# Local attention layers of a three-stage kernel: score products over a stacked high and low part of q, laid out by DMA, and the value matmuls of a tile in one run

## The reference

```python
h = shift_token(x)                       # second half of the features from the token before
q, k, v = jnp.split(h @ wqkv, 3, axis=-1)            # 8 heads of 64
q, k = l2norm(q) * qs, l2norm(k) * ksc
q, k = rotary_xpos(q, k)
# windows of 128 tokens: a query sees the keys of its own window and of the one before
sim = jnp.einsum('bhwid,bhwjd->bhwij', bq * 8, look_around(bk))
attn = softmax(where(mask, -max, sim))
x = x + (attn @ look_around(bv)) @ wo
```

## Time and profile before

| | |
|---|---|
| time, 3 runs | 6484.46, 6486.76, 6487.22 us, median 6486.76 |
| the profiled execution: its own time, its span | 6483.36 us, 6481.6 us |
| mean granted TensorE clock over the span | 0.981 |
| first stage | 0 to 3577 us |
| local attention of layer 0 and 1 | 3577 to 4595, 5039 to 6043 us |
| feed-forward of layer 0 and 1 | 4595 to 5039, 6043 to 6481 us |
| TensorE, VectorE, ScalarE, GpSimd busy over the span | 95%, 79%, 59%, 26% |

### The profile page before, as it was taken

The page is one execution under the profiler, slowest core; times in us unless marked ns, Lnnn a source line. Parts: engine busy times, 40 slices in busy tenths (PEclk is TensorE's granted clock), DMA queues, the critical chain, the costliest instruction groups (busy, mean ns, idle before and its releaser), DMA issues. The chain is left out here.

```text
span 6481.6 us, 108848 instructions
## 1 busy us (share of the span) xinstructions
PE 6166.7 (95%) x41920; PEld 3444.3 (53%) x42112; DVE 5091.6 (79%) x10817; ACT 3803.7 (59%) x6226; POOL 1699.0 (26%) x1259
## 2 busy tenths in 40 slices
PE   6999999999999999999999799999899899999899
PEld 2333333333333333333233688888788688888788
DVE  5877888877888878888886788888666788888666
ACT  1666665666656666656666566666333566666332
POOL 3011000001000100000000577777100577777111
PEclk7999999999999999999999899999999899999999
DMA  2001101111001110010000100000100100000111
GB/s 84 21 29 34 33 16 40 31 29 36 21 30 31 34 32 26 21 37 21 16 16 19 39 15 13 15 14 10 28 11 4 34 15 14 13 15 9 54 50 43
DMA packets 161677, 170.60 MB, mean 26 GB/s; under 512 B 26844, under 2 KB 146436, under 8 KB 161156
## 3 DMA queue, kind: packets, MB, share of 16 engines
q1 hardware_dynamic: 161156, 163.62, 8.9%
HBM read 104.04 MB, written 41.94 MB: 23 GB/s over the span
## 5 line engine op out<-in xcount | busy, mean ns | idle before, releaser
L533 ACT ACTIVATE a_pr<-a_w 128x1024 f32<-128x1024 f32 x2048 | 2078.4, 1024 | 1145.4 <-PE a_w L421 825.8
L637 DVE TENSOR_REDUCE a_mx<-a_b 128x1 f32<-128x512 f32 x2688 | 1740.2, 685 | 326.5 <-PE a_b L405 307.4
L405 PE MATMUL a_b<-a_kp,a_qp 96*128 96x512 bf16 x4096 | 1445.2, 387 | 111.7 <-DVE a_mx L637 48.6
L421 PE MATMUL a_w<-a_qp,a_kp 99*128 99x512 bf16 x4096 | 1225.3, 380 | 33.7 <-ACT a_pr L533 33.6
L635 DVE CUSTOM_DVE_ANT_0 a_junk<-a_b,a_gw 128x512 bf16<-128x512 f32 x1408 | 965.7, 686 | 246.6 <-PE a_b L405 206.9
L452 PE MATMUL a_po<-a_pr,a_v 128*17 128x512 f32 x8192 | 1067.8, 594 | 0.5 <-ACT a_pr L533 0.5
L405 PEld LDWEIGHTS a_b<-a_kp,a_qp 96*128 96x128 bf16 x4096 | 335.3, 97 | 1255.5 <-issue 701.1
L1378 POOL TENSOR_TENSOR l_p<-l_p,l_rc 128x512 f32<-128x512 f32 (+1 forms) x512 | 632.5, 1254 | 450.8 <-DVE l_rc L1291 450.8
L1185 ACT ACTIVATE l_p<-l_S,l_nm 128x256 f32<-128x256 f32 (+1 forms) x1024 | 467.8, 466 | 457.8 <-DVE l_nm L1283 457.6
L421 PEld LDWEIGHTS a_w<-a_qp,a_kp 99*128 99x128 bf16 x4096 | 388.3, 98 | 521.3 <-ACT a_pr L533 110.8
L1034 PE MATMUL l_G<-l_wqkv,l_hT 128*128 128x512 f32 x2304 | 606.9, 408 | 22.0 <-DVE l_wqkv L1323 9.5
(11 more groups left out here) (163 smaller groups left out, 8222.0 us busy)
## 6 DMA issues: line engine op xcount, KB each, us to landing
a_qp<-q_parts SPq DMA_DIRECT2D x384, 64.0 KB, 2.3
a_kp<-k_parts SPq DMA_DIRECT2D x384, 64.0 KB, 2.2
a_xc<-in_x SPq DMA_DIRECT2D x32, 512.0 KB
l_tab<-in_rotary SPq DMA_DIRECT2D x128, 128.0 KB, 2.1
q_parts<-a_stage SPq DMA_DIRECT2D x32, 384.0 KB, 2.5
k_parts<-a_stage SPq DMA_DIRECT2D x32, 384.0 KB, 2.6
x<-a_xc SPq DMA_DIRECT2D x16, 512.0 KB, 2.9
f_xo<-x SPq DMA_DIRECT2D x16, 512.0 KB
```

Source lines behind the costliest of these rows:

```text
L405: eng.matmul(bk, qp[s][0:96, qb * 128:qb * 128 + 128], kp[s][0:96, c * 512:c * 512 + 512], start=True, stop=True).then_inc(full, 1)
L421: m = eng.matmul(wide[u][:, c * 512:c * 512 + 512], kp[s][0:99, kb * 128:kb * 128 + 128], qp[s][0:99, u * 1024 + c * 512:u * 1024 + c * 51 ...
L533: eng.activation(pr[(2 * n + u) % NP][:, :], wide[u][:, :], ACT.Exp, scale=0.25).then_inc(s_exp[u], 1)
L637: t = eng.tensor_reduce(mx[g % 2][:, qb, c:c + 1], banks[i], X, ALU.max)
```

## The change

Scores: q is laid out anew for each head, its 64 high rows over its 64 low rows (`qs`). The keys are laid out as `kh`, the high part twice, once beside each half of q, and `kl`, the low part beside the high half of q with zeros below it. One matmul with `kh` then gives (high + low) by high, and one with `kl` high by low. Each covers one head and both windows of keys, so a pair of heads takes four matmuls of 256 columns where it took six. Keys of three tiles lie in three slots; where the slots of the two windows come in turned order, `place` says so and a second, turned mask is used.

ScalarE and VectorE now write all of q and k in one instruction each to plain buffers `qT` and `kT` (one of each, not two or three), and SyncE copies them from there to the stacked buffers: `stack(t, 0)` issues 4 DMAs and `stack(t, 1)` issues 6, each of 64 partitions by 4 x 128 numbers (128 KB). `sim` waits for the 4 of q and the 6 of k. `hT` and `oT` are one buffer instead of two.

Values: the four `pv` of a tile now follow `out` at the end of TensorE's step. Output: `out` makes high by high and high by low with 4 matmuls of 512 columns and low by high with 4 of 256 (before 12 of 256), and VectorE adds the two halves to `xs` in two instructions.

```diff
+    qT, kT = [sb(f"qT{k}", [128, 4, 128], F32R) for k in range(2)], [sb(f"kT{k}", [128, 4, 128], F32R) for k in range(2)]
+    qs = [sb(f"qs{i}", [128, 4, 2, 128], F32R) for i in range(2)]
+    kh, kl = (sb(n, [128, 4, 2, 3, 128], F32R) for n in ("kh", "kl"))
...
-            pe.wait_ge(s_ql, t + 1)
-            pe.wait_ge(s_kl, t + 1)
-            for k in ([0, 1] if w else [1]):
-                for x, y in PASSES:
-                    m = eng.matmul(z[:, :, k, :], qT[t % 2][x][:, pair * 128:pair * 128 + 128], kT[(t - 1 + k) % 3][y][:, pair, :, :],
+            pe.wait_ge(s_qs[t % 2], 64 * (t // 2 + 1))
+            pe.wait_ge(s_ks[t % 3], 96 * (t // 3 + 1))
+            slots = [t % 3] if not w else [0, 2] if t % 3 == 0 else [t % 3 - 1, t % 3]
+            step = slots[-1] - slots[0] or 1
+            for x in (kh, kl):
+                for h in range(2):
+                    m = eng.matmul(z[:, h, 0:2, :] if w else z[:, h, 1, :], qs[t % 2][:, pair, h, :],
+                                   x[:, pair, h, slots[0]:slots[-1] + 1:step, :] if w else x[:, pair, h, slots[0], :],
                                    start=False, stop=True, skip_group_check=True)
...
-            for x, z in PASSES:
-                for c in range(4):
-                    m = eng.matmul(G[1][:, 0:D], oT[t % 2][x][:, c * 128:c * 128 + 128], wo[z][:, c, :], start=i == 0, stop=i == 11)
-                    i += 1
+            for c in range(4):
+                eng.matmul(G[1][:, :], oT[0][:, c * 128:c * 128 + 128], wo[:, c, :, :].rearrange("p z n -> p (z n)"),
+                           start=c == 0, stop=True, skip_group_check=True)
+            for c in range(4):
+                m = eng.matmul(G[1][:, 0:D], oT[1][:, c * 128:c * 128 + 128], wo[:, c, 0, :], start=False, stop=True, skip_group_check=True)
...
             on(p_T, n - 3, 1)
-            on(pv, n - 3, 0)
             on(qk_T, n - 1, 1)
             on(p_T, n - 3, 2)
             on(p_T, n - 3, 3)
-            on(pv, n - 3, 1)
             on(sim, n - 2, 3)
             on(x_T, n + 1)
-            on(pv, n - 3, 2)
             on(out, n - 4)
-            on(pv, n - 3, 3)
+            for pair in range(4):
+                on(pv, n - 3, pair)
...
-            eng.tensor_tensor(xs[:, t, :], G[1][:, 0:D], xs[:, t, :], ALU.add).then_inc(s_res, 1)
+            eng.tensor_tensor(xs[:, t, :], G[1][:, 0:D], xs[:, t, :], ALU.add).then_inc(s_half, 1)
+            dve.wait_ge(s_half, t + 1)
+            eng.tensor_tensor(xs[:, t, :], G[1][:, D:2 * D], xs[:, t, :], ALU.add).then_inc(s_res, 1)
...
-        for x in [x for both in kT for x in both]:
-            m = eng.tensor_scalar(x[:, :, :, :].rearrange("p a h n -> p (a h) n"), ident[:, :].unsqueeze(1).to_broadcast([128, 8, 128]), 0.0, None, ALU.mult)
+        for o in range(4):
+            m = eng.tensor_scalar(kl[64:128, o, :, :, :].rearrange("p h s n -> p (h s) n"),
+                                  ident[64:128, :].unsqueeze(1).to_broadcast([64, 6, 128]), 0.0, None, ALU.mult)
...
+        def stack(t, n):
+
+            sp.wait_ge(s_kl if n else s_ql, t + 1)
+            if t > 1:
+                sp.wait_ge(s_sim, 4 * (t - 2) + 4)
+            for h in range(2):
+                rows = slice(64 * h, 64 * h + 64)
+                if n:
+                    s = t % 3
+                    for r in range(2):
+                        eng.dma_start(kh[64 * r:64 * r + 64, :, h, s, :].bitcast(F32), kT[0][rows, :, :].bitcast(F32)).then_inc(s_ks[s], 16)
+                    eng.dma_start(kl[0:64, :, h, s, :].bitcast(F32), kT[1][rows, :, :].bitcast(F32)).then_inc(s_ks[s], 16)
+                else:
+                    for r in range(2):
+                        eng.dma_start(qs[t % 2][64 * r:64 * r + 64, :, h, :].bitcast(F32), qT[r][rows, :, :].bitcast(F32)).then_inc(s_qs[t % 2], 16)
...
+            if n:
+                stack(n - 1, 0)
+                stack(n - 1, 1)
             if n + 2 < NT:
                 load_table(n + 2)
```

More of the change, by code:

```diff
@@ L959, in local_layer @@
     wq = [sb(f"wqkv{i}", [128, 2, 3 * HL * DL], F32R) for i in range(2)]
-    wo = [sb(f"wo{i}", [128, 4, D], F32R) for i in range(2)]
+    wo = sb("wo", [128, 4, 2, D], F32R)
     tab = [sb(f"tab{i}", [128, 2, 2, DL]) for i in range(3)]
@@ L963, in local_layer @@
     ident, identb = sb("ident", [128, 128]), sb("identb", [128, 128], BF16)
-    mask = sb("mask", [128, 512], BF16)
+    mask = [sb(f"mask{i}", [128, 2, 2, 128], BF16) for i in range(2)]
     nh = sb("nh", [128, 16])
     sh = [sb(f"sh{i}", [128, 4, 128]) for i in range(2)]
-    hT = [[sb(f"hT{i}{k}", [128, 256], F32R) for k in range(2)] for i in range(2)]
+    hT = [sb(f"hT{k}", [128, 256], F32R) for k in range(2)]
     qk = sb("qk", [128, 2, HL, DL])
@@ L978, in local_layer @@
     pT = [sb(f"pT{i}", [128, 2, 2, 128]) for i in range(4)]
-    oT = [[sb(f"oT{i}{k}", [128, 512], F32R) for k in range(2)] for i in range(2)]
+    oT = [sb(f"oT{k}", [128, 512], F32R) for k in range(2)]
     G = [ph.ps(f"G{i}", [128, 512]) for i in range(2)]
@@ L986, in local_layer @@
     mask32, wraw = sq[:, 0, :, :].rearrange("p h d -> p (h d)"), t1[1][:, :, :, :].rearrange("p a h d -> p (a h d)")
-    wo_flat = [x[:, :, :].rearrange("p a n -> p (a n)") for x in wo]
+    wraw_c = wraw.rearrange("p (c n) -> p c n", n=D)
     s_ident, s_cq, s_cw = ph.sem("ident"), ph.sems("cq", 2), ph.sem("cw")
@@ L999, in local_layer, with place @@
     n_zero = sum(1 for g in range(NT // 4) if 4 * g % W == 0)
+    def place(t, k):
+        return 1 - k if t % W and t % 3 == 0 else k
     def pos(pairs, t, pair):
@@ L1033, in qkv @@
                 for c in range(2):
-                    m = eng.matmul(G[n % 2][:, :], hT[t % 2][x][:, c * 128:c * 128 + 128], wq[z][:, c, n * 512:n * 512 + 512], start=i == 0, stop=i == 5)
+                    m = eng.matmul(G[n % 2][:, :], hT[x][:, c * 128:c * 128 + 128], wq[z][:, c, n * 512:n * 512 + 512], start=i == 0, stop=i == 5)
                     i += 1
@@ L1162, in qk_hi @@
             act.wait_ge(s_qkT, 2 * t + n + 1)
[L1163 to L1173, removed]
+            d, full = (kT, s_kh) if n else (qT, s_qh)
+            if t:
+                if n:
+                    act.wait_ge(s_ks[(t - 1) % 3], 96 * ((t - 1) // 3 + 1))
+                else:
+                    act.wait_ge(s_qs[(t - 1) % 2], 64 * ((t - 1) // 2 + 1))
+            eng.activation(d[0][:, :, :].rearrange("p a n -> p (a n)"), T[:, :], ACT.Copy).then_inc(full, 1)
         def sim(t, pair):
@@ L1329, in vector @@
                 dve.wait_ge(s_cw, 48)
-                eng.tensor_copy(mask[:, :], mask32).then_inc(s_mask, 1)
+                for i in range(2):
+                    for k in range(2):
+                        m = eng.tensor_copy(mask[i][:, :, k, :], mask32.rearrange("p (h k n) -> p h k n", h=2, k=2)[:, :, k ^ i, :])
+                m.then_inc(s_mask, 1)
                 dve.wait_ge(s_woh, 1)
-                eng.tensor_tensor(wo_flat[1], wraw, wo_flat[0].bitcast(F32), ALU.subtract).then_inc(s_wol, 1)
+                eng.tensor_tensor(wo[:, :, 1, :], wraw_c, wo[:, :, 0, :].bitcast(F32), ALU.subtract).then_inc(s_wol, 1)
             on(sim, n - 2, 1)
@@ L1419, in sync @@
         load_wqkv(2)
-        for n in range(NT):
+        for n in range(NT + 1):
             g = (n + 4) // 4
```

50 lines of the change are left out of this document (25 added, 25 removed).

## The result

| | before | after |
|---|---|---|
| median of 4 runs each, us | 6485.61 (6481.80 to 6487.22) | 7171.77 (7168.29 to 7175.56) |
| span of the profiled execution, us | 6481.6 | 7173.8 |
| mean granted clock of TensorE | 0.981 | 0.932 |

The ratio is 1.1059, 95% interval 1.1045 to 1.1073: 10.6% slower, 686 us. The forecast was 6872 us, the range ended at 7080. The sign and the mechanism came as predicted, the size did not: 386 us were forecast, and the measured time lies above the range.

What follows compares the result with a forecast made beforehand. TensorE's stream was taken to set the 15.15 us step, then the chain through k's copies: 12.43 + 4.7 = 17.1 us. 126 x (1.95 + 1.05 for the clock) plus 7 adds 385 us: 6872 us, range 6650 to 7080.

Steps and rivals of the forecast that it cites:

- TensorE's own work falls by 0.94 us a step: Score matmuls per tile go from 24 to 16 at 0.117 us each; TensorE's work falls from 15.15 to 14.21 us.
- `out` gives nothing: Output product on TensorE: the new matmuls take 1.40 us, as the 12 before did, so no gain.
- The chain takes over: From k's landing through `qkv`, ScalarE's copy and VectorE's list to the end of k's low part: 12.43 us.
- T: The moment when a tile's k has landed and its first score products start on TensorE; a turn was forecast at 17.1 us.
- The landing, 4.7 us: SyncE's six DMAs behind the low part of k: 5 x 0.50 + 2.1 + 0.1 us, bounds 3.9 and 6.7.
- the 3.8 us: Cross-check of the landing by the skill's formula: the six copies taken as one transfer of 786 KB.
- The clock, 1.05 us a step: TensorE idles about 2.5 us a step, its clock halves, delaying the chain 1.5 us in 7 of 10 steps.
- my 7 in 10: Share of steps in which TensorE's clock was expected to fall to half after the idle stretch.
- The sum: Over both local layers: 126 x (1.95 + 1.05) plus 7, 385 us more, giving 6872 us, some 5.9% slower.
- Landing is costly: Rival for the six copies of k: issues of 0.70 us, 3.1 to land, 6.7 in all; 7124 us, chance 0.13.
- The clock holds: Rival: TensorE's clock stays up despite the idle stretch, only 1.95 us more a step; 6740 us, chance 0.25.
- hidden: Rival: copies of k stay off the path, TensorE's 14.21 us sets the step; 6369 us, chance 0.05 faster, 0.02 no change.

Runs made afterwards that it cites:

- e7: The kernel before with only the new form of the output product (4 matmuls of 512 columns and 4 of 256): 6483.66 us, ratio 0.9995.
- e3: The changed kernel without the ten copies of a step, scores reading constants and waiting for the low parts of q and k: 6435.25 us, ratio 0.9920.
- e2: The changed kernel with the mask matmul ahead of each step's wait for k issued 18 times instead of once: 6941.02 us, ratio 1.0699.
- e12: The changed kernel without the two copies of the low part of k, its buffer zero, TensorE's work the same: 6824.16 us, ratio 1.0525.
- e10: Stacked scores with two early copies of k instead of six, output matmuls and value order as before the change: 6451.34 us, ratio 0.9945.
- e11: e10 with value matmuls of pairs 1 to 3 in one run ahead of `out`, output added last, `oT` doubled: 6437.00 us, ratio 0.9924.

## Where the prediction failed

The direction and the path were right: the copies of k stand on the chain, and the clock falls behind the wait. Two terms of the sum were too small. The landing was put at 4.7 us and measured 6.10; the clock was put at 1.05 us a step and measured 2.0. The second went wrong because it was priced for an idle stretch of 2.5 us, and the stretch was 4.1.

- **TensorE's own work falls by 0.94 us a step; `out` gives nothing.** `out` was right (e7: 0.9995). For the scores, e3 has a step of 14.80 us with waits of 0.92 and 0.25; 14.80 - 1.17 = 13.63 us of work, against 14.21 forecast. The difference, 0.6, is close to the 0.5 us of the value matmuls' run. So "the `pv` are as many as before" was true of their number, but not of their cost.
- **The chain takes over, 12.43 us from T to the low part of k at full clock.** Right: 4.06 to `qk_T` (e2) plus 8.30 makes 12.4.
- **The landing, 4.7 us.** The first term that was mis-sized: 6.10. One issue was taken as 0.50 and is 0.66 with its gap, so five of them are 3.35 us instead of 2.5; last issue to T 2.73 instead of 2.2. I had set the price of an issue by rows of single DMAs, the table's 0.33, and there it isn't seen what a copy costs behind others: the table itself takes 0.60 in that place. The landing behind an issue is dearer too: the first copy, with none ahead of it, already needs 2.42 us, where the table had 2.1. The data too took longer than the 33 ns a piece of the earlier trace rows: 0.96 busy at 194 GB/s is 16 x 0.96 x 512 bytes / 194 GB/s = 41 ns; but that moved the landing of the sixth copy by under 0.2 us against the first. The value lies within the bounds of 3.9 to 6.7 given then. The Trainium skill, page "DMA: Bandwidth & Descriptors", section "Anatomy of one DMA", gives the fit behind the 3.8 us for DMAs that GpSimd issues; those here are SyncE's. The 3.8 us are below all that was measured for six copies, 5.58 to 6.25, and the rate in the fit is 436 GB/s, where the cuts behind the issues have 194 to 264.
- **The clock, 1.05 us a step.** The second term that was mis-sized: 2.0 us, in nearly each step (e2). I took the stretch without work as 2.5 us; it is 4.1 us in the mean, 1.4 more by the landing and 0.2 more because TensorE's list ends earlier, the value matmuls being cheaper. For stretches of 2.5 us my 7 in 10 was too high: in e12 the clock was down behind 22 of 95 waits up to 2.75 us. So the second miss follows from the first: a longer wait took the clock down in each step, at a price of 2.0 us where I had 1.5. e12 has the landing that was forecast, 4.73 us, and there the clock costs 0.6 us a step: with it the sum would give 6872 - 126 x 0.45 = 6815, of 6824 measured. The 1.05 was thus too small for the kernel as it is, and too large for the landing it stood beside.
- **The sum.** 1.40 us for landing, 1.03 for the clock and -0.16 for the rest make 2.27 us a step, 126 x 2.27 = 286. 6872 + 286 = 7158, of 7172 measured.
- **The rivals.** "Landing is costly" (7124, 0.13) had the right landing within 0.6 us and the clock's price at half; it came nearest. "The clock holds" was wrong, "hidden" needed a landing below 2.7 us and was wrong by 3.4 us a step. The range ended at 7080, 44 us short of even the costly case, and that case joined the dearer landing with the same 1.05 us of clock; a longer wait makes both dearer at once.

## What to carry to other kernels

A layout by DMA between the maker and the reader of a value costs, on the path, an issue for each copy (0.66 us here) and 2.5 to 2.7 us behind the last: before changing the layout, count the copies that stand between the last write and the first read, and have those begun that don't need the last write (e10: two copies of what exists early, instead of six behind what comes last, 7172 against 6451 us). If TensorE will wait in each step, price the clock together with the wait, as one term that grows with it. And where the wait for a copy is taken away, look for the wait that comes next: three different kernels ended at a step of 14.8 us, each time with TensorE waiting for VectorE once or twice a step.

## What the runs showed of the hardware that I had not expected

- **A copy's issue depends on what is in the queue.** 128 KB: 0.62 us with 512-byte pieces behind others, 0.60 with 2 KB pieces (0.46 for the first of a step); the table's 0.33 becomes 0.60 in that place.
- **Matmuls of one kind in one run are cheaper.** The 16 value matmuls of a step (x32): 1.94 us in one run, 2.4 in four.
- **The clock's loss falls behind the wait.** The granted clock fell to 0.50 by 4215, with TensorE idle since 4212.4, and work began at 4216.38; it was 1.00 again only at 4221.5. The first matmuls behind the wait pay. In 22 of the 60 steps read in the first layer the clock fell only 0.3 to 1.3 us after work had begun again, so that a clock of 1.00 at the end of a wait is no sign that it will hold.
- **VectorE beside GpSimd.** The same 128x1024 operation (`scale`) takes 1.22 us where GpSimd is idle and 2.08 where GpSimd's three normalising multiplications stand beside it. GpSimd in the kernel after, with VectorE idle, and in e10, with VectorE at work:

```profile
4213.71 3.03 POOL L1387 TENSOR_TENSOR l_p<-l_p,l_rc 128x512 f32<-128x512 f32 x3
```

```profile
4165.97 4.02 POOL L1397 TENSOR_TENSOR l_p<-l_p,l_rc 128x512 f32<-128x512 f32 x3
```

  Both engines are longer when together, by 0.86 and by 1.0 us. The Trainium skill, page "GPSIMD Engine Reference", section "Specifications", lists the SBUF interfaces of GpSimd as shared with VectorE, with contention where VectorE has two SBUF inputs; `scale` reads two tensors in SBUF, and the rows agree. Not every row is that clear: in e3 `scale` begins beside the same three multiplications and takes 1.30, and `rotate` behind it 1.80. It may be why e3, e10 and e11 end at the same 14.8 us; no run took GpSimd's work away, so this is argued, not shown.
